# The turned tile's rest subtracted one slot later, and the next exponential taken before its high half

## The reference

```python
# layer 0, per image: theta, phi are 64 x 1024, g is the image itself
f = softmax(einsum('ndq,ndk->nqk', theta, phi) / sqrt(64));  attn = einsum('nqk,nck->ncq', f, g)
x = x + conv1x1(attn, W_fuse)
# layer 1, on x: group norm in 32 groups, then q, k, v of 128 channels
h = group_norm(x);  scores = einsum('bic,bcj->bij', q(h), k(h)) * 128 ** -0.5
x = x + conv1x1(einsum('bcj,bij->bci', v(h), softmax(scores)), p_w)
```

## Time and profile before

| | us |
|---|---|
| median of 3 runs | 1777.76 (1776.36 to 1781.32) |
| the profiled execution's own time | 1780.63 |
| its span in the trace | 1778.8 |
| busy PE / DVE / ACT / POOL | 1686.0 / 1414.7 / 1399.3 / 1442.2 |
| transfers' share of 16 engines' span | 81.4% |

### The profile page before, as it was taken

How to read it: one execution, slowest core, us unless ns; L and a number is a source line. 1 busy time by engine, 2 the same in 40 slices (tenths; PEclk the granted TensorE clock), 3 DMA queues, 4 the chain that set the end, 5 groups by cost and what they waited for, 6 DMA issues and landing times.

```text
span 1778.8 us, 34679 instructions
## 1 busy us (share of the span) xinstructions
PE 1686.0 (95%) x8970; PEld 1112.1 (63%) x8970; DVE 1414.7 (80%) x1605; ACT 1399.3 (79%) x2088; POOL 1442.2 (81%) x1513
## 2 busy tenths in 40 slices
PE   4799999999999999999999999999999999999986
PEld 3466666666666666666666666666666666666653
DVE  5588878888888888888888888788888888888864
ACT  3488878778888778888888888788888887888864
POOL 3589878888888889888889888889888888888863
PEclk9799999999999999999999999999999999999999
DMA  2589888788888888888888888888888888878874
GB/s 63 105 150 168 166 164 174 161 167 171 163 175 168 169 163 173 168 175 162 172 162 165 176 169 169 166 160 167 178 167 170 174 160 167 175 160 176 161 143 101
DMA packets 860086, 286.33 MB, mean 161 GB/s; under 512 B 822304, under 2 KB 823200, under 8 KB 860064
## 3 DMA queue, kind: packets, MB, share of 16 engines
q1 hardware_dynamic: 860064, 286.08, 81.4%
HBM read 50.86 MB, written 17.04 MB: 38 GB/s over the span
## 4 chain that ended last, share of the span: by engine, by line
PE 66%; issue 13%; DVE 8%; ACT 7%; POOL 2%; DMA 1%; ACTq 0%; SPq 0%; DVEq 0%; POOLq 0%
PE o_ps L447 26%; PE s_ps L447 22%; PE m_ps L447 11%; PE s_ps L487 7%; DVE neg_max L753 3%; DVE pair L770 2%; ACT e L652 2%; ACT s_ps L652 2%; ACT h_hi L631 1%; DVE stats L817 1%; ACT et L662 1%; DMA et<-pair 1%; DVE den_scaled L782 1%; DVE x L807 0%; DVE theta L841 0%
## 5 line engine op out<-in xcount | busy, mean ns | idle before, releaser
L447 PE MATMUL o_ps<-et,v_hi 128*128 128x512 f16 x2048 | 696.6, 382 | 28.3 <-issue 18.2
L753 DVE TENSOR_REDUCE neg_max<-s_ps 128x1 f32<-128x1024 f32 x512 | 624.7, 1220 | 98.2 <-PE s_ps L447 96.4
L447 PE MATMUL o_ps<-et,v_lo 128*128 128x512 f16 x1024 | 389.8, 381 | 0.0
L447 PEld LDWEIGHTS o_ps<-et,v_hi 128*128 128x128 f16 x2048 | 202.9, 99 | 269.8 <-issue 78.4
L447 PE MATMUL s_ps<-phi,theta 128*128 128x512 f32 x1024 | 332.1, 447 | 12.5 <-ACT e_copied L652 4.8
L770 DVE SCALAR_TENSOR_TENSOR pair<-s_ps,pair 128x1024 f16<-128x1024 f32 x256 | 311.9, 1218 | 38.5 <-ACT pair L677 38.1
L652 ACT ACTIVATE s_ps<-s_ps,neg_max 128x1024 f32<-128x1024 f32 x256 | 278.1, 1086 | 53.1 <-DVE neg_max L753 49.6
L907 POOL TENSOR_TENSOR pair<-e_copied,pair 128x1024 f16<-128x1024 f32 x128 | 274.1, 2141 | 22.2 <-ACT pair L675 22.2
L764 DVE SCALAR_TENSOR_TENSOR et<-s_ps,et 128x1024 f16<-128x1024 f32 x128 | 156.8, 1225 | 153.9 <-ACT et L662 153.9
L677 ACT ACTIVATE pair<-s_ps 128x1024 f16<-128x1024 f32 x256 | 261.9, 1023 | 17.6
L447 PE MATMUL s_ps<-k_hi,q_hi 128*128 128x512 f32 x512 | 248.9, 486 | 5.0 <-POOL q_lo L907 2.1
(11 more groups left out here) (132 smaller groups left out, 2937.3 us busy)
## 6 DMA issues: line engine op xcount, KB each, us to landing
rden_row<-rden_dram SPq DMA_DIRECT2D x128, 256.0 KB, 3.9
xs<-in_x SPq DMA_DIRECT2D x32, 512.0 KB, 4.7
phi<-phi SPq DMA_DIRECT2D x64, 256.0 KB, 3.1
out_y<-y_sb SPq DMA_DIRECT2D x64, 256.0 KB, 3.4
et<-pair SPq DMA_TRANSPOSE x384, 4.5
rden_dram<-rden SPq DMA_DIRECT2D x128, 2.0 KB, 2.2
w_f<-in_w_fuse_t SPq DMA_DIRECT2D x1, 64.0 KB, 2.7
ident_sb<-in_ident SPq DMA_DIRECT2D x1, 64.0 KB, 2.3
```

The lines of the kernel that those rows point to most:

```text
L447: mm = pe.matmul(out, lhs_t, rhs, start=start and n == 0, stop=stop and n == len(terms) - 1)
L753: nc.vector.tensor_reduce(neg_max[:, t % 4:t % 4 + 1], s_ps[:, part(t), :], AX.X, ALU.max, negate=True).then_inc(s_max, 1)
```

## The change

On ScalarE the calls for slot s change places: the exponential of tile s-1 now comes ahead of the high half of the turned tile s-2. They meet in slots 1, 5, 9 and 13. On VectorE `take_lo` is split: the low half of a crossed tile stays where it was; that of a turned tile moves one slot later (t = s-3 in place of s-2), from slots 1, 5, 9, 13 to slots 2, 6, 10, 14, and stands there between the maxima and `normalised`. Operations, operands and waits are the same.

```diff
 # ScalarE
                 for s in range(SLOTS):
+                    exponentials(it, s)
                     turned_hi(it, s)
-                    exponentials(it, s)
                     pair_hi(it, s)
...
 # VectorE
-            def take_lo(it, s):
-                t = s - 2
-                if not here(tile_at, it, t) or here(copied_at, it, t):
-                    return
-                r = t % GROUP
+            def turned_lo(it, s):
+                t = s - 3
                 if here(turned_at, it, t):
...
-                    return
+
+            def pair_lo(it, s):
+                t = s - 2
+                if not here(crossed_at, it, t):
+                    return
+                r = t % GROUP
...
                     maxima(it, s)
+                    turned_lo(it, s)
                     normalised(it, s)
-                    take_lo(it, s)
+                    pair_lo(it, s)
                     reciprocals(it, s)
```

## The result

| | before | changed |
|---|---|---|
| median | 1777.06 us (1774.97 to 1781.32, 4 runs) | 1820.75 us (1817.83 to 1821.55, 4 runs) |
| the profiled execution, its span | 1780.63, 1778.8 | 1817.83, 1816.0 |
| PE / DVE / ACT / POOL busy | 1686.0 / 1414.7 / 1399.3 / 1442.2 | 1690.9 / 1415.3 / 1390.8 / 1443.8 |

The ratio is 1.0239, with a 95% interval from 1.0225 to 1.0253: 43.7 us slower, 2.4%. Forecast were 1822 us and 2.5%.

A forecast was written before the change was run, and what follows sets the result against it. TensorE was taken to bound the kernel. Delays of 0.92 us in slot 14 and 0.50 in slot 10, over 31 images, add 44.0 us to 1777.8: 1822 us, 2.5% slower, range 1800 to 1834.

The forecast's parts named there:

- What bounds the kernel: TensorE, idle only 35.4 us in the steady stretch at full clock; idle growth below 30 us would refute the forecast.
- Slot 14: Low half ahead of the normalising delays it 0.94 us, reaching TensorE through slot 0's turn; 0.92 us per image as mean.
- the second chain: From slot 14's normalising through GpSimd's subtraction and SP's transposes to slot 2's value product: same 0.94 us, not paid twice.
- Slot 10: Normalising ends at 907.16 and the value product starts at 907.30, not 906.80: a new 0.50 us wait per image.
- Slots 2 and 6: Added low half costs nothing: transfer wait covers slot 2, slot 6 about in time; 0.1 kept for the range.
- L782 leaves the place ahead of the maxima and the normalising: Reciprocals' instruction, held up by GpSimd, no longer precedes them; gain is the 1.6 us L807 cost TensorE.
- slot 4 might gain: ScalarE's earlier group norm steps could shorten the turns' waits in slot 4, at most 11 us; nothing taken.
- The sum: 31 x (0.92 + 0.50) = 44.0 us added per execution, median 1821.8, say 1822 us, 2.5% slower.
- The rule weighed: Two-SBUF-input VectorE and SBUF-reading GpSimd instructions exclude each other: L782 held, low half and normalising not; gain 1.6 us.
- The gain by an earlier exponential: Rival: the copied tile's exponential no longer waits behind the high half, saving some 20 idle us: 1758; chance 4%.
- only one of the two is paid: Rival: slot 14's delay only, 28.5 us, 1806, or slot 10's only, 15.5 us, 1793; together 13%.
- More than both: Rival: TensorE also meets later transfers around slots 15 and 0, or 6 and 2: 12 us, 1834; chance 12%.

The follow-up runs named there:

- Tile 11 alone: Both parts of the change applied only to turned tile 11 (low half in slot 14), against the kernel before: 1805.87 us, ratio 1.0169.
- giving it back: Against the kernel changed for tile 11 only, slot 14's low half put behind the normalising: 1800.79 us, ratio 1.0140 to the kernel before.
- covering the first: Against the changed kernel, TensorE in slot 0 does the value product ahead of the turn: 1822.61 us, ratio 1.0265 to the kernel before.
- tile 7 alone: Both parts of the change applied only to turned tile 7 (low half in slot 10), against the kernel before: 1791.15 us, ratio 1.0087.
- tiles 15 and 3 alone: Both parts of the change applied only to tiles 15 and 3 (low half in slots 2 and 6), against the kernel before: 1773.31 us, ratio 0.9984.

## Why the prediction was right

**What bounds the kernel.** Right: TensorE's idle time rose from 35.4 to 70.9 us in the steady stretch, forecast were at least 30 more, and the granted clock stayed at full speed there.

**Slot 14.** 0.92 us per image were forecast, and slot 0 grew from 3.83 to 4.73 us. Tile 11 alone cost 29.7 us, the term says 28.5. Normalising starts 2.27 us after the maxima, summed were 2.28, and over 28 images 2.31 us after slot 13's scores where it was 1.41: 0.90 later. The 5.41 us behind it have no slack: the 0.29 us at their end moved along. That the second chain carries the same delay, and is not paid again, is shown from both sides: giving it back emptied slots 2 and 6, and covering the first brought the wait back in slot 2.

**Slot 10.** 0.50 us forecast, slot 10 grew by 0.47; tile 7 alone cost 15.0 us, the term says 15.5. The latency of 0.14 us from a single row of before held in every image (0.15).

**Slots 2 and 6.** "I count nothing" was nearly right for the total, but it hides two things. In slot 6 the normalising starts 0.31 us later in an image with VectorE in time, as estimated; it does not end when the product wants to start but 0.14 us too late. Against that stands a gain, for tiles 15 and 3 alone 3.5 us net. Its source was seen in the prediction (L782 leaves the place ahead of the maxima and the normalising), but priced at the 1.6 us that L807 cost TensorE by the list. It was worth more, 7.5 us when it was done by itself. This is the term that was mis-sized: the list names the engine that waited last, and half of what the late VectorE cost stood there as the turn's wait for the exponential in slot 4. The prediction saw that slot 4 might gain, took nothing for it, and put it down to ScalarE's group norm steps; it gained 0.13 us, by VectorE's earlier maxima.

**The sum.** That 44.0 us met 43.7 so closely has some luck in it. Tiles 11, 7 and the pair 15 and 3, each by itself, cost 29.7 + 15.0 - 3.5 = 41.2 us; their intervals of 2 to 4 us allow the 43.7, and the gain of 3.5 was left out of the forecast.

**The rule weighed.** What the prediction drew from the Trainium skill ("SBUF — State Buffer", section "Who interferes with whom") stands: L782 is held by GpSimd wherever it is put, 642 ns in the mean in one place and 446 in the other, while the low half kept its duration in the new place. In the kernel before 89 of its 128 cases last over 250 ns, each with a GpSimd instruction beside it, and 63 of them end within 40 ns of that instruction; the 35 with none beside them are all short.

**The rivals.** The gain by an earlier exponential is out: with VectorE's move alone the time is the same within 2 us. Of "only one of the two is paid" both halves were run and both are paid. "More than both" did not come.

## What to carry to other kernels

An engine's idle time ahead of a moved instruction does not tell what the move is worth; measure the time from the moment its inputs are there to the moment somebody waits for what stands behind it, place by place. The same move cost 30 us in one place of the loop and 15 in another, and gained 3.5 in two others together. Where one instruction's delay runs along two chains, count it once, and expect little from hiding only the wait that the profile shows. And a small instruction that another engine can hold up belongs into idle time, not ahead of the one that the path runs through: that alone gave 0.4%.

## What the runs showed of the hardware

- The low half with one input in PSUM lasted 1211 to 1225 ns in its new place (1223 to 1226 before), beside a GpSimd instruction in 123 of 128 cases, while the four-column L782 with two inputs in SBUF took 211 ns at the least, 1303 at the most, and rose from 446 to 642 ns in the mean when it was moved.
- Where the loop turns, VectorE is idle for 0.29 us between two instructions, and the profile puts it down to issue or to TensorE, as it falls.
- Ahead of the value product of slot 2 the profile wrote "issue" (1.02 us before, 1.49 with the turn's wait covered), where the product started 0.18 to 0.36 us after the third transposing transfer had landed.
- In the run with the turn behind the values the granted clock fell to 1.2 GHz in five images, each time with a slot 2 that a wait had made 5.6 us or longer, but not with every such slot (two of 6.0 us had none); the slot behind it grew by 0.55 to 1.02 us.
